# Two attentions: scores taken twice, by rows and transposed, with minus the row maximum as rows of the contraction

## The reference, cut to what matters

```python
# stage at0: layer norm, rotary position embedding, causal softmax
xn = (x - mean) / sqrt(var + 1e-5) * g + b
q, k, v = split(xn @ Wqkv + bqkv)          # heads of 8 lanes
q, k = q * cos + rotate_half(q) * sin, k * cos + rotate_half(k) * sin
y = x + softmax(causal(q @ k.T / sqrt(8))) @ v @ Wo + bo
# stage at1: rms norm, no embedding, no mask, no biases
y = x + softmax(q @ k.T / sqrt(8)) @ v @ wo
```

## Time and profile before

| | us |
|---|---|
| three runs: median | 3088.99 |
| three runs: lowest, highest | 3088.39, 3092.74 |
| the profiled execution, time | 3087.34 |
| the profiled execution, span | 3085.6 |
| of it stage `at0` (first DMA issue to last DVE instruction) | 12.8 to 347.5 |
| of it stage `at1` (the same) | 768.0 to 1112.2 |

### The profile page before, as it was taken

The page is one execution under the profiler, slowest core; times in us unless marked ns, Lnnn a source line. Parts: engine busy times, 40 slices in busy tenths (PEclk is TensorE's granted clock), DMA queues, the critical chain, the costliest instruction groups (busy, mean ns, idle before and its releaser), DMA issues. The chain is left out here.

```text
span 3085.6 us, 50804 instructions
## 1 busy us (share of the span) xinstructions
PE 2272.7 (74%) x20075; PEld 1438.8 (47%) x20075; DVE 2193.2 (71%) x3826; ACT 1553.5 (50%) x2527; POOL 1420.6 (46%) x1127
## 2 busy tenths in 40 slices
PE   4888766765677759989868998999999975552703
PEld 2555445543455535556534545545545543342303
DVE  4777555886677635555536889888889884888698
ACT  4888425553677742222226666665676652221460
POOL 5555243555322200000006988988988992322001
PEclk9999887887799989999989999999999997665856
DMA  1000000000000010000012222222222220000000
GB/s 40 1 2 2 9 30 18 16 17 5 1 2 1 2 47 1 1 1 1 1 33 70 87 74 70 87 74 70 87 73 70 83 70 28 18 14 8 0 0 28
DMA packets 109916, 95.52 MB, mean 31 GB/s; under 512 B 12256, under 2 KB 106352, under 8 KB 109552
## 3 DMA queue, kind: packets, MB, share of 16 engines
q1 hardware_dynamic: 109680, 92.26, 9.8%
...
## 5 line engine op out<-in xcount | busy, mean ns | idle before, releaser
L1939 POOL TENSOR_TENSOR mam_h<-mam_h,mam_c_all 128x1024 f32<-128x1024 f32 x256 | 658.8, 2591 | 88.9 <-DVE mam_h L2011 88.9
L2011 DVE TENSOR_TENSOR_SCAN mam_h<-mam_decay,mam_ps_b 128x1024 f32<-128x1024 f32 x256 | 574.6, 2275 | 98.2 <-PE mam_ps_b L1642 96.2
L1642 PEld LDWEIGHTS mam_ps_b<-mam_diag,mam_duT 64*128 64x128 f32 x4096 | 251.3, 190 | 219.1 <-DVE mam_h L2011 130.5
L1833 ACT ACTIVATE mam_decay<-mam_delta,mam_a_neg 128x508 f32<-128x508 f32 x512 | 331.3, 710 | 32.8 <-DVE mam_h L2011 28.6
L1642 PE MATMUL mam_ps_b<-mam_diag,mam_duT 64*128 64x128 f32 x4096 | 297.0, 287 | 54.8 <-DVE mam_h L2011 42.9
L1661 PE MATMUL mam_ps_y<-mam_h,all_ident 64*64 64x512 f32 x2048 | 255.8, 615 | 13.9 <-POOL mam_h L1939 13.9
L519 DVE TENSOR_REDUCE at_top<-at_ps_s 128x4 f32<-128x512 f32 x256 | 174.9, 683 | 121.0 <-PE at_ps_s L359 120.9
L1234 ACT ACTIVATE moe_silu<-moe_ps_g 128x512 f32<-128x512 f32 x144 | 86.0, 597 | 287.2 <-PE moe_ps_g L1181 261.0
L437 ACT COPY at_probT<-at_ps_t 128x512 f32<-128x512 f32 x256 | 145.1, 589 | 119.9 <-PE at_ps_t L344 119.7
L198 POOL TENSOR_TENSOR at_parts_rest<-at_qk,at_parts 128x256 f32<-128x256 f32 x64 | 42.9, 670 | 319.4 <-ACT at_parts L193 319.4
L1184 PE MATMUL moe_ps_u<-moe_ynT,moe_w_up 128*128 128x512 f32 x288 | 157.8, 631 | 36.0 <-DVE moe_hidden L1317 36.0
...
## 6 DMA issues: line engine op xcount, KB each, us to landing
mam_c_all<-mam_c_rows SPq DMA_DIRECT2D x256, 256.0 KB, 3.4
all_x_all<-in_x SPq DMA_DIRECT2D x8, 256.0 KB, 4.6
ret_xg<-all_x_all SPq DMA_DIRECT2D x32, 64.0 KB, 1.8
ret_ctx<-in_ctx SPq DMA_DIRECT2D x32, 64.0 KB, 2.0
mam_xg<-all_x_all SPq DMA_DIRECT2D x8, 256.0 KB, 4.1
xat_xg<-all_x_all SPq DMA_DIRECT2D x8, 256.0 KB, 2.4
xat_ctx<-in_ctx SPq DMA_DIRECT2D x8, 256.0 KB, 3.0
out<-qua_res SPq DMA_DIRECT2D x8, 256.0 KB, 2.3
```

The lines of the kernel that those rows point to most:

```text
L1642: last = nc.tensor.matmul(ps_b[:, slot, odd, :, at // 2, x:x + HT], duT[r, d, s % DT, at, :], diag[r, chunk % SLOTS, at, :, :], start=True ...
L1833: last = nc.scalar.activation(decay[:, s % SLOTS, :, n, :, 1:T], src, ACT.Exp, scale=a_neg[:, d, s % DT, st:st + 1])
L1939: nc.gpsimd.tensor_tensor(flat(h[:, slot, :, :, :, :]), flat(h[:, slot, :, :, :, :]), flat(c_all[:, chunk, :, :, :, :]), ALU.mult).then_in ...
L2011: nc.vector.tensor_tensor_scan(row(h[:, s % H_SLOTS, :, :, :, :]), row(decay[:, s % SLOTS, :, :, :, :]), row(ps_b[:, s % 2, :, :, :, :]), ...
```

## The change

`attention` is written anew for both stages; nothing else of the program changes but its weights' order in DRAM. The parts of it:

- **Scores twice.** The scores are computed once by rows into `ps_s` (queries down the partitions, as before), only to find the maximum, and four steps later (`LAG_E`) once more transposed into `ps_e` (keys down the partitions). Both tiles have two banks, eight heads: a batch is done in two halves (`x` = 0, 1). Both times `at0` adds its mask by matmul (L476).
- **Minus the maximum in the contraction.** k's tile `k64` has ones in three further rows of each row half, and q's tile `q64` has minus the maximum there, split in three bfloat16 parts. So `ps_e` comes out already shifted, and ACT takes the exponential straight from PSUM into `e` (`exponentiate`, 128x1024), keys down the partitions, as the product with `v_wide` needs it. The subtraction on DVE, the 16 transposes of probabilities and their four copies on ACT are gone.
- **The way of the maximum.** DVE finds it in one instruction for half a batch (`find_top`, 128x1024). POOL splits it (`split_top`, four instructions of 128x16), TensorE turns and negates it (`turn_top`), ACT copies it (`copy_top`), SP writes it to DRAM (`write_top`) and, once it has landed, reads it into the rows of `q64` (`read_top`, two DMAs of 3 rows).
- **q and k by lanes, four batches at once.** The projections put lanes down the partitions (L451, 512 columns, float32; in `at0` four of them per group, since the rotated half is projected too, in `at1` two). The rotary embedding is done there by DVE (`turn_half`) and POOL (`add_halves`); ACT and POOL split q and k into three bfloat16 parts (`split_first` to `split_third`).
- **Through DRAM into slots.** SP writes the parts of a group to DRAM (`write_split`) and reads them back into `q64` and `k64` in the order of the six products (`read_rows`: 6 DMAs for q of 24, 16 and 8 rows, 12 for k of 8 rows; a row is 8 KB). The 16 turns of parts and their two copies are gone. `q64` and `k64` have a ring of three groups (`RING`), and q and k are prepared up to two groups ahead (`LEAD`).
- v is projected, and the output computed, by groups of four batches.

All engines walk through the same steps `s`, one per batch; `n` is the group and `r` the batch in it.

```diff
--- before.py
+++ after.py
...
-            def turn_probabilities(i, b, n):
-                for j in range(NJ):
-                    pe.wait_ge(exp_ready, (i * G + b) * NJ + j + 1)
-                    turn(n + j, j % 2, lambda k: prob[:, b % 2, j, k, :])
...
-            def shift(steps, i, b, banks):
-
-                for j in banks:
-                    dve.wait_ge(scores_ready, (i * G + b) * NJ + j + 1)
-                    src = ps_s[:, j, :, :]
-                    steps.then(nc.vector.tensor_reduce(top[:, b % 2, j, :], src, AX_X, ALU.max))
-                    steps.settle()
-                    nc.vector.tensor_tensor(prob[:, b % 2, j, :, :], src, spread(top[:, b % 2, j, :], T), ALU.subtract)\
-                        .then_inc(shifted, 1)
...
+        LAG_E, LAG_V, LAG_U, LAG_O, LEAD = 4, 5, 6, 2, 2
+        FIRST, LAST = -LEAD * G, B + 2 * G
+        PREPARED = 4
+        RUNS = (((0, 0, 3), (3, 0, 2), (5, 0, 1)), ((0, 0, 1), (1, 0, 1), (2, 0, 1), (3, 1, 1), (4, 1, 1), (5, 2, 1)))
+        LANDS = [len(runs) for runs in RUNS]
...
+            def write_split(n, which):
+
+                sp.wait_ge(third_ready[which], n + 1)
+                if n > 0:
+                    sp.wait_ge(landed[which][(n - 1) % RING], 16 * 2 * LANDS[which] * ((n - 1) // RING + 1))
+                for r in range(2):
+                    dst = rows_dram[which, r].rearrange("n d (a t) -> (d a) n t", a=PAIRS)
+                    sp.dma_start(dst, split[r * HALF:(r + 1) * HALF, which, :, :]).then_inc(written[which], 16)
+
+            def read_rows(n, which, halves):
+
+                slot = n % RING
+                sp.wait_ge(written[which], 16 * 2 * (n + 1))
+                if n >= RING:
+                    sp.wait_ge(e_filled, 2 * 2 * (n - RING + 1) * G)
+                for r in halves:
+                    rows = (q64, k64)[which][r * HALF:(r + 1) * HALF, slot, :, :].rearrange("p a t -> p (a t)")
+                    for at, first, count in RUNS[which]:
+                        src = rows_dram[which, r, first:first + count].rearrange("n d a -> (n d) a")
+                        sp.dma_start(rows[at * HD:(at + count) * HD, :], src).then_inc(landed[which][slot], 16)
+
+            def write_top(b):
+
+                bank, at = AT[("t", b)]
+                sp.wait_ge(taken[bank], at + 1)
+                if b >= 2:
+                    sp.wait_ge(top_landed[b % 2], 16 * 2 * (b // 2))
+                sp.dma_start(tops_dram[b % 2].rearrange("n r a t -> (n r a) t"), topT[:, b % 2, :]).then_inc(top_written[b % 2], 16)
+
+            def read_top(b):
+
+                slot, cols = slot_of(b)
+                sp.wait_ge(top_written[b % 2], 16 * (b // 2 + 1))
+                for r in range(2):
+                    row = r * HALF + SLOTS * HD
+                    sp.dma_start(q64[row:row + NS, slot, :, cols], tops_dram[b % 2, :, r, :, :]).then_inc(top_landed[b % 2], 16)
+
+            for s in range(FIRST, LAST + 1):
+                n, r = s // G, s % G
+                if r == 3 and whole(n + LEAD):
+                    write_split(n + LEAD, 0)
+                if r == 0 and whole(n + 1):
+                    write_split(n + 1, 1)
+                if batch(s - 1):
+                    write_top(s - 1)
+                    read_top(s - 1)
+                if r == 0 and whole(n + 1):
+                    read_rows(n + 1, 0, (0, 1))
+                if r in (1, 2) and whole(n + 1):
+                    read_rows(n + 1, 1, (r - 1,))
 
         ALL_LOADED = 16 * p["n_loads"]
 
         @block.tensor
...
+            def scores_free(b, x):
+                slot, cols = slot_of(b)
+                if x == 0 and b % G == 0:
+                    for which in range(2):
+                        pe.wait_ge(landed[which][slot], 16 * 2 * LANDS[which] * (b // G // RING + 1))
+                if b > 0 or x > 0:
+                    pe.wait_ge(top_ready, 2 * b + x)
+
+            def exponents_free(b, x):
+                if x == 0:
+                    pe.wait_ge(top_landed[b % 2], 16 * 2 * (b // 2 + 1))
+                if b > 0 or x > 0:
+                    pe.wait_ge(e_ready, 2 * b + x)
+
+            def masks(b, x, dst, stationary, moving):
+                for r in range(2):
+                    nc.tensor.matmul(dst[:, r, :, :], stationary[:], repeat(moving[:], NJ), start=True, stop=False, skip_group_check=True)
+
+            def products(b, x, dst, left, right, rows, done):
+                slot, cols = slot_of(b)
+                for j in range(NJ):
+                    for r in range(2):
+                        at = slice(r * HALF, r * HALF + rows)
+                        last = nc.tensor.matmul(dst[:, r, j, :], left[at, slot, NJ * x + j, cols], right[at, slot, NJ * x + j, cols],
+                                                start=(not rope and j == 0), stop=(j == NJ - 1), skip_group_check=True)
+                        if j == NJ - 1:
+                            last.then_inc(done, 1)
+
+            def both(s, x):
+
+                now, then = batch(s), batch(s - LAG_E)
+                if now:
+                    scores_free(s, x)
                     if rope:
-                        for j in (2 * two, 2 * two + 1):
-                            nc.tensor.matmul(ps_s[:, j, :, :], c.ident_b[:], repeat(c.causal_b[:], NK), start=True, stop=False, skip_group_check=True)
-                    for k in range(NK):
-                        for j in (2 * two, 2 * two + 1):
-                            r = slice(j % 2 * parts.HALF, j % 2 * parts.HALF + parts.ROWS)
-                            last = nc.tensor.matmul(ps_s[:, j, k, :], parts.qT[r, b % 2, NK * two + k, :], parts.kT[r, b % 2, NK * two + k, :],
-                                                    start=(not rope and k == 0), stop=(k == NK - 1), skip_group_check=True)
-                            if k == NK - 1:
-                                last.then_inc(scores_ready, 1)
-
-            def turn_probabilities(i, b, n):
...
+                    turn_x(n + LEAD)
+                if r == 2 and come:
+                    project("k", n + LEAD, NP // 2)
+                    if rope:
+                        project("kr", n + LEAD, 3)
+                both(s, 0)
+                if r == 1 and come:
+                    project("q", n + LEAD, 0)
+                    if rope:
+                        project("qr", n + LEAD, 1)
+                if r == 2 and go:
+                    turn_att(n - LAG_O)
+                if batch(s - LAG_V):
+                    values(s - LAG_V)
+                if batch(s - 1):
+                    turn_top(s - 1)
+                both(s, 1)
+                if r == 3 and go:
+                    output(n - LAG_O)
+                if r == 0 and whole(n - 1):
+                    values_in(n - 1)
+                if batch(s - LAG_U):
+                    turn_back(s - LAG_U)
...
+            def exponentiate(b, x):
+                act.wait_ge(e_filled, (2 * b + x + 1) * 2)
+                if x == 0 and b >= 2:
+                    act.wait_ge(pv_ready, b - 1)
+                nc.scalar.activation(e[:, b % 2, 2 * x:2 * x + 2, :, :].rearrange("p k j t -> p (k j t)"), ps_e[:].rearrange("p r j t -> p (r j t)"),
+                                     ACT.Exp, scale=HD ** -0.5).then_inc(e_ready, 1)
...
+            def split_top(b):
+                pool.wait_ge(top_ready, 2 * b + 2)
+                if b >= 2:
+                    bank, at = AT[("t", b - 2)]
+                    pool.wait_ge(filled[bank], at + 1)
+                whole_top = top[:, b % 2, :, :].rearrange("p r a -> p (r a)")
+                nc.gpsimd.tensor_copy(top_split[:, b % 2, 0, :], whole_top).then_inc(top_step, 1)
+                pool.wait_ge(top_step, 3 * b + 1)
+                nc.gpsimd.tensor_tensor(top_rest[:], whole_top, top_split[:, b % 2, 0, :], ALU.subtract).then_inc(top_step, 1)
+                pool.wait_ge(top_step, 3 * b + 2)
+                nc.gpsimd.tensor_copy(top_split[:, b % 2, 1, :], top_rest[:]).then_inc(top_step, 1)
+                pool.wait_ge(top_step, 3 * b + 3)
+                nc.gpsimd.tensor_tensor(top_split[:, b % 2, 2, :], top_rest[:], top_split[:, b % 2, 1, :], ALU.subtract).then_inc(split_ready, 1)
...
+            def find_top(b, x):
+                dve.wait_ge(s_ready, (2 * b + x + 1) * 2)
+                if x == 0 and b >= 2:
+                    dve.wait_ge(split_ready, b - 1)
+                nc.vector.tensor_reduce(top[:, b % 2, :, NJ * x:NJ * x + NJ], ps_s[:], AX_X, ALU.max).then_inc(top_ready, 1)
...
+            def turn_half(name, n, which, part):
+                if n > 0 and part == 0:
+                    dve.wait_ge(compact_ready[which], n)
+                bank, at = AT[(name, n)]
+                dve.wait_ge(filled[bank], at + 1)
+                lanes = lambda t: t.rearrange("p (g t) -> p g t", g=G)
+                dst, table = ((straight, cosT), (turned, sinT))[part]
```

(2 more changed lines are left out.)

570 lines of the change are left out of this document (332 added, 238 removed).

## The result

| | before | after |
|---|---|---|
| median of the runs side by side, us | 3088.69 (3088.19 to 3092.74, 4 runs) | 3034.63 (3031.75 to 3040.77, 4 runs) |
| span of the profiled execution, us | 3085.6 | 3033.8 |

A forecast was written before the change was run, and what follows sets the result against it. It took PE and DVE by turns to bound `at0` and SP's DMA chain `at1`: 3087.3 less 70 saved in `at0` and 107.6 in `at1` is 2909.7, or 2911 us on the median's level; range 2875 to 2980.

The forecast's parts named there:

- A `write_top`'s landing 2.0, the last rows of k 2.5: SP's chain: tops' writes land in 2.0 us, k's last rows in 2.5, giving 24.2 us per group in `at1`.
- sign of "wrong": Something the profile would show if the forecast failed, here row reads landing over 5 us after issue.
- The last line of the prediction: Each 0.5 us of a `write_top`'s landing costs 1.5 us per group, 10 us in `at1`.
- the starts: Each stage's work before first scores: these come at 51.3 us instead of 39.9 in `at0`, 803.6 instead of 792.6 in `at1`.
- transfers slower: Rival, chance 0.24: landings of 3.2 and 3.4 us make SP the bound of both stages, total 2965 us.
- Issuing 0.47 apart: SP issues its 34 DMAs per group in order, 0.47 us apart.
- 26.0 us per group of `at0`: Pace of `at0` from PE and DVE by turns: 20.6 us plus additions, 6.5 per batch.
- some 16: Time PE and DVE would need per group of `at1`, in us, without masks and rotated projections.
- 2.58: Half a batch of `at0` in us: handover 0.06, four masks 0.88, products 0.40, 0.03, maximum 1.21.
- The turns of PE and DVE: In `at0` PE's masks and products and DVE's maximum alternate, as `ps_s` has one buffer: 5.16 us a batch.
- The clock as a rival at 0.03: Rival, chance 0.03: PE's clock stays at half, 47 us per group in `at0`, 30 in `at1`, total 3110.
- costed "at nothing": The transfers themselves, in both stages, were given no cost in the forecast.

The follow-up runs named there:

- the late reads: The changed kernel with SP issuing the reads of the tops (row maxima) behind the row reads instead of before them: 2954.12 us, ratio 0.9577.
- no DMA: The changed kernel without any DMA inside the two stages, `q64` filled with 0 once per stage: 2951.66 us, ratio 0.957.
- only the norm moved: Changed kernel with tops' reads behind row reads and k in 6 DMAs, plus DVE's norm between step 0's two maxima: 2917.78 us, ratio 0.9465.
- the reordered kernel: On tops' reads late, 6 k reads, norm early: x turned and q, k projected behind both score halves, `k64` filled by slot: 2900.26 us.
- without DMAs in the new order: The reordered kernel without any DMA in the two stages' loops, `q64` filled with 0: 2894.11 us, ratio 0.9385.
- late fill: The changed kernel with DVE filling only the first slot of `k64` before the start, the others in the third and fourth step: 3012.66 us.

## Why the prediction was wrong

- **"A `write_top`'s landing 2.0, the last rows of k 2.5"** is the step that cost most. I took the queue as not crowded. Alone on it the tops land in 1.4, behind row reads in 4 to 6.6 (median 4.3 in the middle of `at1`), and the last rows of k took 5.2 (922.4 to 927.6), over the 5 us that the prediction named as a sign of "wrong". The last line of the prediction put 10 us in `at1` on each 0.5 of landing; the late reads gave back 216.6 - 165.4 = 51 us there and 28 in `at0`. Of the miss, this chain is the 50 us of `at1` and some 25 of `at0` (after less no DMA), the engines' own pace in `at0` some 27 (204.2 - 176.7), and the starts 20. The rival "transfers slower" had this mechanism, but took its landings from rows of unlike transfers (3.2 and 3.4) and so ended at 2965.
- **"Issuing 0.47 apart"** was too high: 0.33 for a row read. It hid a part of the landing's error.
- **26.0 us per group of `at0`**, which I took as the engines' own pace, was 31.2 in the order as written, and **"some 16" in `at1`**, which I had not worked out, was 22.3 to 24.6. Missing was PE's wait for the norm at the head of step 1, 2.25 us idle, with the scores of that step behind it, and the lower clock after it; I had counted the norm as DVE's work at step 0 and not looked at who reads it. The granted clock was 0.94 in the middle of `at0` even without DMAs, and 1.00 once the wait was gone. The wait cost 2.7 and the clock 1.4 in a group. With only the norm moved, 27.2 remains at full clock, 1.2 over my sum: a half batch without further work takes 2.72 to 2.77 instead of 2.58, and the halves that share PE with projections or turning `att` 4.56, 3.73 and 3.29 instead of 4.06, 3.5 and 2.73. The 26.3 of the reordered kernel is near the forecast's 26.0 by luck: my sum was for another order. In `at1` 18.6 to 20.5 remains without DMAs in the new order; ACT, which the prediction called hidden in `at0`, is busy 75 us of 100 there.
- **The turns of PE and DVE**, four masks, products, maximum, one behind the other, were right in mechanism, and in size within 7%.
- **The starts** were 11 and 10 us off: in `at0` the fill began 3 us later than I had it and took 10.30 where I had 7.3 (my upper bound was 10.4), ACT's table took 1.28, and the first 12 row reads of k landed 7 us after the last was issued instead of 2.3. The late fill gave 15 us, but by taking two thirds of the fill out of the chain, most of which the forecast had priced; it does not measure how far the fill's price was off. The Trainium skill (VectorE: DVE Perf Modes, Zero memsets can be issued as uint32) says that a fill takes one cycle per element, whatever its type, and that one of zeros over 2-byte elements can go by 4 bytes; the rows below agree in that both fills take 0.84 ns per element, of 2 or of 4 bytes. My 0.59 came from an operation that is not a fill.
- **The clock as a rival at 0.03** did not decide, but it was at work throughout: 0.91 in the middle of `at0` and 0.78 in that of `at1`, where PE waits at each group's start, against 0.99 and 0.89 in the two stages before. A wait costs its length and can cost, behind it, work at the lower of the two levels (1.2 instead of 2.4 GHz). The products with the values show it (two rows of after's timeline, the first just behind a wait of 6.75 us for k's rows, the second one step on):

```profile
990.93 1.94 PE L515 MATMUL at_ps_o<-at_e,at_v_wide 128*32 128x128 f32 x32
...
996.72 1.08 PE L515 MATMUL at_ps_o<-at_e,at_v_wide 128*32 128x128 f32 x32
```

- **The transfers themselves, costed "at nothing"**: that held for the engines' instructions (the maximum takes 1224 ns on average in `at0` with DMAs, 1225 without) and failed on the queue.

Left open: how the row reads spread over the 16 DMA engines, and why `at1` reordered still has groups of 22.5 beside some of 19.8.
